# Where VectorE forms two low parts of the softmax weights, and the order of two jobs on GpSimd, in a two-layer cross-attention kernel

## Chip, core and metric

The kernel runs on one core of a Trainium2 chip. The metric is the device time of one execution in microseconds (us), from launch to end. The engines are TensorE (PE in the profile; its weight loads are PEld), VectorE (DVE), ScalarE (ACT), GpSimd (POOL) and SyncE (SP), which issues the DMAs.

## What is computed

Two transformer layers over x (8 batches x 512 tokens x 256). The change lies in the first attention of the second layer, a self-attention with 16 heads of 64:

```python
def _attn(xq, xc, Wq, Wk, Wv, Wo, bo):
    q = (xq @ Wq).reshape(B, N, HEADS, D_HEAD)
    k = (xc @ Wk).reshape(B, S, HEADS, D_HEAD)
    v = (xc @ Wv).reshape(B, S, HEADS, D_HEAD)
    scores = jnp.einsum("bnhd,bshd->bhns", q, k) * D_HEAD ** (-0.5)
    attn = jax.nn.softmax(scores, axis=-1)
    out = jnp.einsum("bhns,bshd->bnhd", attn, v).reshape(B, N, HEADS * D_HEAD)
    return out @ Wo + bo

x = _attn(_ln(x, g1, b1), _ln(x, g1, b1), Wq1, Wk1, Wv1, Wo1, bo1) + x      # L1, first attention
```

B is 8, N and S are 512, HEADS is 16, D_HEAD is 64. Before it runs layer L0 (cross-attention and an MLP), after it a second attention against the context and a gated MLP.

## The kernel before

**Precision.** Matmul operands are split in two: a rounded high part (`pool_copy` L159 on GpSimd or `act_copy` L156 on ScalarE) and a low part, source minus high part (`dve_rest` L162 on VectorE, `pool_rest` L165 on GpSimd). `mm3` (L146, L147, L148) sums high x high, high x low and low x high.

**Stage.** The self-attention is one software pipeline, `loop3`: s runs from -1 to 67, and N3 = 64 is the number of pairs of heads (8 batches x 8 pairs; pair p of batch b is step 8b + p). Step s works on three pairs: it projects pair u = s+1, forms scores and exponentials of pair t = s, and multiplies the weights of pair d = s-1 with the values. A step has four parts, j = 0 to 3. In part j the keys of block j (128 of 512) are handled: TensorE writes the scores of both heads (128 x 1024), ScalarE takes the exponential into one of two buffers, `pst3[j % 2]` (`exponent`, L1530), the high part goes to `P3[0][:, j]` and the low part to `P3[1][:, j]`. GpSimd rounds blocks 0 and 3, ScalarE blocks 1 and 2. VectorE's `rests(n)` forms the low part of block n = 4t + j; it reads two SBUF tensors of 128 x 1024 and signals `p3_lo`. The exponential of block n waits for `rests(n - 2)`, since it writes the same buffer; TensorE's `values(d, j)` waits for `rests(4d + j)`, and the next block's scores on TensorE wait for the exponential.

Also in step s, for pair u = s+1:

- j = 0: TensorE projects the queries (`project(u, 0)`, into bank 2) and the keys (`project(u, 1)`, bank 3). ScalarE copies the queries of head 0, takes exponential 4s, copies the queries of head 1, then the keys of each head. VectorE forms the low parts of queries (L1599, two instructions, the second after ScalarE's copy for head 1) and of keys (L1603, two). GpSimd copies the high keys once more (`k3_dup`, two copies 64 x 512).
- j = 1: values projected (`project_v`); ScalarE rounds them, VectorE's `value(u)` forms their low part from PSUM (128 x 256, two instructions).
- the row maxima: for each of four query blocks TensorE writes plain scores, and VectorE reduces them (`largest`, L1618, 128 x 1024 in PSUM, four in a step). On VectorE the order is block 0 in j = 1, blocks 1 and 2 in j = 2, block 3 in j = 3. On TensorE block 2 waits for the maximum of block 0 and block 3 for that of block 1, for their banks; block 1 waits for the low values; block 0 waits for the low keys.

For finished pairs: SyncE brings the sums of the exponentials of pair s-2 together, VectorE takes the reciprocal (L1647, in j = 0), and SyncE spreads it through DRAM. In j = 2 GpSimd multiplies the output of pair s-2 by it (L1734), rounds it (L159, 128 x 512) and forms its low part (L165, signal `o3_lo`). In j = 3 TensorE's `output` applies the output weights to half of the tokens for two pairs, into bank 2: it waits for `b3_max` of block 2 (whose maxima stood in banks 2 and 3), and in odd steps also for the `o3_lo` of the same step. VectorE adds the result to x (L1666), then bank 2 is free for the next `project(u, 0)`. In step p = 4 VectorE also takes the statistics of the next batch's layer norm, in p = 5 it scales, and in p = 6 TensorE transposes (L152; after the maximum of block 1), ScalarE applies the affine part, and GpSimd splits the result (`ln_split_pool`) before the next projection.

**Order.** Each engine executes its instructions in the order of the program; semaphores join the engines. The order is written by hand in `dve_attention1`, `pool_attention1` and the like.

Of the kernel before, what the change touches and what calls it, by code (L numbers as in the profile page):

```python
# [110 lines left out]
def build(nc, x, ctx_in, par, con, bias, wts, out):  # L111
    es = ExitStack()
    with es:  # L113
# [262 lines left out]
        def ok(v, n):  # L376
            return 0 <= v < n
# [925 lines left out]
        def out3_at(s, j):  # L1303

            e, half = (s - 2, 0) if s % 2 else (s - 3, 1)
            return [(e, half)] if ok(e, N3) and j == (1 if half and e >= N3 - 3 else 3) else []
# [285 lines left out]
        def dve_attention1():  # L1592
            def project(u, n):
                i, src = u % 2, bank(2 + n)
                for h in range(2):
                    hs = src[64 * h:64 * h + 64, :]
                    if n == 0:
                        dve.wait_ge(q3_hi, 2 * u + h)
                        nc.vector.tensor_tensor(qb[i][h][top, :], hs, f32(qa[i][h])[top, :], ALU.subtract  # L1599
                                                ).then_inc(q3_lo.sem, 1)  # L1600
                    else:
                        dve.wait_ge(k3_hi, 2 * u + h)
                        nc.vector.tensor_tensor(ka[i][h][low, :], hs, f32(ka[i][h])[top, :], ALU.subtract  # L1603
                                                ).then_inc(k3_lo.sem, 1)

            def rests(n):
                if 0 <= n < 4 * N3:
                    if n % 4 in (1, 2):
                        dve.wait_ge(p3_act, 2 * (n // 4) + n % 4 - 1)
                    else:  # L1610
                        dve.wait_ge(p3_pool, 2 * (n // 4) + n % 4 // 3)
                    dve_rest(P3[1][:, n % 4, :], pst3[n % 2], P3[0][:, n % 4, :]).then_inc(p3_lo.sem, 1)

            def largest(u, q, b0):
                dve.wait_ge(b3_mm, 4 * u + q)
                dve.wait_ge(nm3_mm, u - 1)
                dve.wait_ge(m3_set, 0)
                nc.vector.tensor_reduce(M3[:, q, 0:128:64], bank(b0, 2).rearrange("p (a b) -> p a b", a=2),  # L1618
                                        AX.X, ALU.max).then_inc(b3_max.sem, 1)

            def value(u):
                s_ = v3_s[(u // 2) % 2]
                src = bank(v3_bank(u)).rearrange("p (t a e) -> p t a e", t=2, a=2)
                tt = slice(2 * (u % 2), 2 * (u % 2) + 2)
                dve.wait_ge(v3_hi, u)
                for c in range(2):
                    cs = slice(128 * c, 128 * c + 64)
                    m = dve_rest(s_[1][:, tt, :, cs], src[:, :, :, 64 * c:64 * c + 64], s_[0][:, tt, :, cs])
                m.then_inc(v3_lo.sem, 1)

            ahead = dve_attention2()
            for s in loop3:
                t, u, d = s, s + 1, s - 1
                b, p = divmod(max(t, 0), 8)
                more = ok(t, N3)
                if s == 0:
                    after_attention0(dve)
                for j in range(4):
                    if j == 0:
                        rests(4 * s - 1)  # L1640
                    if ok(u, N3) and j == 0:
                        project(u, 0)
                    if ok(d - 1, N3) and j == 0:
                        k, i = (d - 1) % 2, (d - 1) // 2
                        dve.wait_ge(sum3[k], 2 * i + 1)
                        dve.wait_ge(out3[k], i - 1)
                        nc.vector.reciprocal(SR3[k], SQ3[k]).then_inc(rec3.sem, 1)  # L1647
                    if ok(u, N3) and j == 0:
                        project(u, 1)
                    if j == 1:  # L1650
                        rests(4 * s)
                    if s == 0 and j == 1:
                        value(0)
                    if ok(u, N3) and u > 0 and j == 1:
                        value(u)
                    if ok(u, N3) and j >= 2:
                        largest(u, 2 * j - 3, odd_bank(u))
                    if j == 2 or j == 3 and not out3_at(s, j):
                        rests(4 * s + j - 1)
                    for e, half in out3_at(s, j):  # L1660
                        xv = xbuf(2, e // 8)[:, 2 * half:2 * half + 2, :]
                        dve.wait_ge(o3_mm, e - 1 + half)
                        dve.wait_ge(x_bias, 16 + e // 8)
                        if e % 8 > 1:
                            dve.wait_ge(o3_add, e - 3 + half)
                        nc.vector.tensor_tensor(xv, bank(out3_bank(e, j)).rearrange("p (a c) -> p a c", a=2), xv, ALU.add  # L1666
                                                ).then_inc(o3_add.sem, 1)
                        if j == 3:
                            rests(4 * s + 2)
                    if ok(u, N3) and j in (1, 2):  # L1670
                        largest(u, 2 * j - 2, 2)
                    for job in weights3_at(s, j):
                        dve_weight_rest(job)
                    for _ in range(early4.get(tail3(s, j), 0)):
                        next(ahead)
                    if more and j == 3 and p == 4:
                        ln_x_stats(*after3(b))
                    if s < 0:
                        yield s
                if more and p == 5:  # L1680
                    ln_scale(18 + b, xbuf(*after3(b)), C)
            for _ in ahead:
                pass

        def pool_attention1():
# [1 line left out]
                nc.gpsimd.memset(f32(v3_s[i][0][:, :, :, 64:128]), 1.0)  # L1687
                nc.gpsimd.memset(f32(v3_s[i][1][:, :, :, 64:128]), 0.0).then_inc(v3_set.sem, 1)

            def rounded(t, j):  # L1690
                pool.wait_ge(e3, 4 * t + j)
                pool.wait_ge(d3_mm, 4 * (t - 1) + j)
                pool_copy(P3[0][:, j, :], pst3[j % 2]).then_inc(p3_pool.sem, 1)

            pool.wait_ge(x_out[x_at(0, 3)], store_no[0, 3])
            nc.gpsimd.memset(M3, 0.0).then_inc(m3_set.sem, 1)
            pool.wait_ge(o0_mm, 2 * NB - 1)
# [15 lines left out]
            for s in loop3:  # L1713
                t, u, d = s, s + 1, s - 1
                b, p = divmod(max(t, 0), 8)
                more = ok(t, N3)
                if s == 0:
                    after_attention0(pool)
                    ones(1)
                if s == 2:  # L1720
                    for b_ in (6, 7):
                        pool.wait_ge(x_out[x_at(0, b_)], store_no[0, b_])
                for j in range(4):
                    if ok(t, N3) and j == 0:
                        rounded(t, 0)
                    if ok(u, N3) and j == 0:
                        for h in range(2):
                            pool.wait_ge(k3_hi, 2 * u + h)
                            pool_copy(kb[u % 2][h][top, :], f32(ka[u % 2][h])[top, :]).then_inc(k3_dup.sem, 1)
                    if ok(d - 1, N3) and j == 2:  # L1730
                        f = d - 1
                        pool.wait_ge(in3[f % 2], 2 * (f // 2) + 1)
                        pool.wait_ge(d3_out, f)
                        nc.gpsimd.tensor_tensor(OA, OA, RS3, ALU.mult).then_inc(mul3.sem, 1)  # L1734
                        pool.wait_ge(mul3, f)
                        pool.wait_ge(o3_mm, 2 * ((f - 4) // 2) + 1)
                        pool_copy(o3_s[f % 4][0], OA).then_inc(o3_hi.sem, 1)
                        pool.wait_ge(o3_hi, f)
                        pool_rest(o3_s[f % 4][1], OA, o3_s[f % 4][0]).then_inc(o3_lo.sem, 1)
                    if ok(t, N3) and j == 3:  # L1740
                        rounded(t, 3)
                    for job in weights3_at(s, j):
                        pool_weight(job)
                    for _ in range(early4_pool.get(tail3(s, j), 0)):
                        next(ahead)
                    if j == 2 and more and p == 6:
                        pool.wait_ge(v3_mm, 8 * (b - 1) + 7)
                        ln_split_pool(18 + b, ns[(b + 1) % 2])
                    if more and j == 0 and p == 5:
                        ln_pool_rstd(18 + b)  # L1750
                    if s < 0:
                        yield s
                if more and p == 5:
                    ln_add(pool, *after3(b))
# [421 lines left out]
```

## Time and profile before

| | |
|---|---|
| time, median of 3 | 2228.43 us (2227.48 to 2229.39) |
| profiled execution | 2228.43 us, its span 2226.6 us |
| busy share over the span | PE 94%, PEld 80%, DVE 72%, ACT 67%, POOL 46% |
| mean granted TensorE clock | 0.985 of full speed |
| the self-attention stage | about 547 to 1690 us of the span |

The span runs from the first to the last instruction; the profiled execution's own time is 1.8 us more than its span. PE busy counts overlapping matmuls as one stretch. "Idle before" in a row is the time that the engine stood still ahead of the instruction, and the arrow names what released it.

### The profile page before, as it was taken

What the parts mean: (1) busy time and instruction counts of PE and PEld (TensorE: products, weight loads), DVE (VectorE), ACT (ScalarE), POOL (GpSimd) and SP (SyncE); (2) the same over time, 40 slices, a digit from 0 to 9 for tenths busy, and PEclk for the clock granted to TensorE, in tenths of its full rate; (3) what the DMA queues carried; (4) which work ended last, traced back from release to release, by engine and by line L of the source; (5) the groups of instructions that cost most, each with busy time, mean ns of one, the idle gap of its engine ahead of it and who ended that gap; (6) DMA issues with size and microseconds to landing.
All of it is one profiled execution on the core that took longest, in us unless ns stands there. A gap on an engine that the chain in (4) does not pass through costs nothing. (4 is left out here: it accounts for less than half of the span.)

```text
span 2226.6 us, 31299 instructions
## 1 busy us (share of the span) xinstructions
PE 2100.8 (94%) x11628; PEld 1777.8 (80%) x11628; DVE 1606.0 (72%) x2349; ACT 1486.7 (67%) x2157; POOL 1020.8 (46%) x830
## 2 busy tenths in 40 slices
PE   6868999999999999999999999999997799999998
PEld 4656888887778888888788888887876689898887
DVE  5567677665887878878878778887785866666543
ACT  5546788766778777777777777777774355455431
POOL 2146444440354454444544545345454666655422
PEclk9978999999999999999999999999999899999999
DMA  6910000011000100101001010010014411111000
GB/s 193 327 44 8 22 22 22 11 67 48 22 25 16 34 15 15 39 16 34 15 16 34 15 34 15 20 34 15 25 27 180 149 39 57 43 53 48 10 10 20
DMA packets 84280, 102.67 MB, mean 46 GB/s; under 512 B 29664, under 2 KB 61152, under 8 KB 83616
## 3 DMA queue, kind: packets, MB, share of 16 engines
q1 hardware_dynamic: 84128, 100.66, 13.9%
q8 instruction: 93, 1.52, 0.3%
q14 instruction: 59, 0.48, 0.1%
HBM read 65.50 MB, written 33.82 MB: 45 GB/s over the span
## 5 line engine op out<-in xcount | busy, mean ns | idle before, releaser
L146 PE MATMUL PS<-R 128*128 128x256 f32 (+1 forms) x2944 | 1025.3, 348 | 70.3 <-DVE R L162 23.9
L148 PE MATMUL PS<-R 128*128 128x256 f32 (+1 forms) x2944 | 995.7, 338 | 0.0
L147 PE MATMUL PS<-R 128*128 128x256 f32 (+1 forms) x2944 | 995.4, 338 | 0.0
L146 PEld LDWEIGHTS PS<-R 128*128 128x128 f32 x2944 | 562.9, 191 | 187.5 <-issue 53.4
L156 ACT ACTIVATE R<-PS 64x512 fp32r<-64x512 f32 (+4 forms) x860 | 459.7, 547 | 259.4 <-PE PS L1840 131.0
L148 PEld LDWEIGHTS PS<-R 128*128 128x128 f32 x2944 | 562.7, 191 | 60.3
L147 PEld LDWEIGHTS PS<-R 128*128 128x128 f32 x2944 | 563.5, 191 | 54.6
L159 POOL TENSOR_SCALAR R<-F 128x512 fp32r<-128x512 f32 (+1 forms) x293 | 304.1, 1039 | 454.2 <-ACT F L1530 275.2
L162 DVE TENSOR_TENSOR R<-F,R 128x1024 fp32r<-128x1024 f32 (+2 forms) x418 | 458.4, 1110 | 40.8 <-POOL R L159 24.0
L1618 DVE TENSOR_REDUCE F<-PS 128x2 f32<-128x1024 f32 x256 | 301.4, 1214 | 11.2 <-PE PS L1421 10.9
L1530 ACT ACTIVATE F<-PS 128x1024 f32<-128x1024 f32 x256 | 263.0, 1027 | 48.9 <-DVE R L162 27.0
L162 DVE TENSOR_TENSOR R<-PS,R 128x512 fp32r<-128x512 f32 (+3 forms) x348 | 180.8, 542 | 142.3 <-ACT R L156 139.7
L156 ACT ACTIVATE R<-F 128x1024 fp32r<-128x1024 f32 (+2 forms) x248 | 202.9, 832 | 103.3 <-PE PS L148 98.9
L165 POOL TENSOR_TENSOR R<-F,R 128x512 fp32r<-128x512 f32 (+2 forms) x124 | 195.8, 1581 | 24.2 <-ACT R L156 15.7
L156 ACT ACTIVATE F<-PS 64x512 f32<-64x512 f32 (+3 forms) x280 | 160.1, 593 | 69.9 <-PE PS L148 57.5
L1734 POOL TENSOR_TENSOR F<-F 128x512 f32<-128x512 f32 x64 | 87.6, 1369 | 246.7 <-DMA F<-sd 246.7
L1599 DVE TENSOR_TENSOR R<-PS,R 64x512 fp32r<-64x512 f32 x128 | 87.9, 687 | 125.7 <-ACT R L156 125.7
L1383 PE MATMUL PS<-R 128*128 128x512 f32 x512 | 165.6, 404 | 1.4 <-ACT R L156 1.4
L1421 PE MATMUL PS<-R 128*128 128x512 f32 x512 | 160.4, 395 | 6.9 <-ACT F L156 4.9
L1387 PE MATMUL PS<-R 128*128 128x512 f32 x512 | 159.8, 393 | 2.7 <-ACT R L156 2.7
L1170 POOL TENSOR_TENSOR F<-F 128x1024 f32<-128x1024 f32 x32 | 68.0, 2123 | 157.9 <-DVE F L1069 157.6
L1997 DVE SCALAR_TENSOR_TENSOR F<-PS,F 128x512 f32<-128x512 f32 x64 | 47.8, 747 | 102.8 <-PE PS L148 59.1
(92 smaller groups left out, 2032.7 us busy)
## 6 DMA issues: line engine op xcount, KB each, us to landing
F<-sd SPq DMA_DIRECT2D x128, 128.0 KB, 2.9
xs<-F SPq DMA_DIRECT2D x16, 512.0 KB, 3.5
F<-xs SPq DMA_DIRECT2D x16, 512.0 KB, 3.5
gd<-F SPq DMA_DIRECT2D x8, 768.0 KB, 3.9
vd<-F SPq DMA_DIRECT2D x8, 768.0 KB, 6.4
R<-gd SPq DMA_DIRECT2D x6, 1024.0 KB, 5.6
R<-vd SPq DMA_DIRECT2D x6, 1024.0 KB, 5.6
F<-in_x SPq DMA_DIRECT2D x8, 512.0 KB, 5.5
```

What stands on the lines that cost most here:

```text
L146: nc.tensor.matmul(o, L[0], Rr[0], start=start, stop=False, skip_group_check=share)
L147: nc.tensor.matmul(o, L[0], Rr[1], start=False, stop=False, skip_group_check=share)
L148: return nc.tensor.matmul(o, L[1], Rr[0], start=False, stop=stop, skip_group_check=share)
L156: return nc.scalar.activation(o, i, ACT.Identity, **k)
L159: return nc.gpsimd.tensor_scalar(o, i, 1.0, 1.0, ALU.mult, ALU.mult)
L162: return nc.vector.tensor_tensor(o, i, f32(hi), ALU.subtract)
L165: return nc.gpsimd.tensor_tensor(o, i, f32(hi), ALU.subtract)
L1383: nc.tensor.matmul(bank(h), ka[i][h][:, kk], qa[i][h], start=True, stop=False)
L1387: m = nc.tensor.matmul(bank(h), kb[i][h][:, kk], qb[i][h], start=False, stop=True)
L1421: m = nc.tensor.matmul(bank(b0 + h), qa[i][h][:, 128 * q:128 * q + 128], ka[i][h], start=True, stop=True)
L1530: nc.scalar.activation(pst3[n % 2], bank(0, 2), ACT.Exp, scale=0.125).then_inc(e3.sem, 1)
L1618: nc.vector.tensor_reduce(M3[:, q, 0:128:64], bank(b0, 2).rearrange("p (a b) -> p a b", a=2), AX.X, ALU.max).then_inc(b3_max.sem, 1)
```

## The change

On VectorE, in part j = 0, `rests(4s - 1)` no longer comes first: it comes after `project(u, 0)` and the reciprocal, ahead of `project(u, 1)`. In part j = 1 `rests(4s)` no longer comes ahead of `value(u)` but after it, ahead of the first `largest`. On GpSimd the helper `rounded` is written out in place, and the rounding of block 0 comes after the two copies of the keys instead of ahead of them. The number of instructions and all waits stay the same.

```diff
@@ dve_attention1 @@
                 for j in range(4):
-                    if j == 0:
-                        rests(4 * s - 1)
                     if ok(u, N3) and j == 0:
                         project(u, 0)
                     if ok(d - 1, N3) and j == 0:
...
                         nc.vector.reciprocal(SR3[k], SQ3[k]).then_inc(rec3.sem, 1)
+                    if j == 0:
+                        rests(4 * s - 1)
                     if ok(u, N3) and j == 0:
                         project(u, 1)
-                    if j == 1:
-                        rests(4 * s)
                     if s == 0 and j == 1:
                         value(0)
                     if ok(u, N3) and u > 0 and j == 1:
                         value(u)
                     if ok(u, N3) and j >= 2:
                         largest(u, 2 * j - 3, odd_bank(u))
-                    if j == 2 or j == 3 and not out3_at(s, j):
+                    if j in (1, 2) or j == 3 and not out3_at(s, j):
                         rests(4 * s + j - 1)
@@ pool_attention1 @@
-            def rounded(t, j):
-                pool.wait_ge(e3, 4 * t + j)
-                pool.wait_ge(d3_mm, 4 * (t - 1) + j)
-                pool_copy(P3[0][:, j, :], pst3[j % 2]).then_inc(p3_pool.sem, 1)
@@
                 for j in range(4):
-                    if ok(t, N3) and j == 0:
-                        rounded(t, 0)
                     if ok(u, N3) and j == 0:
                         for h in range(2):
                             pool.wait_ge(k3_hi, 2 * u + h)
                             pool_copy(kb[u % 2][h][top, :], f32(ka[u % 2][h])[top, :]).then_inc(k3_dup.sem, 1)
...
-                    if ok(t, N3) and j == 3:
-                        rounded(t, 3)
+                    if ok(t, N3) and j in (0, 3):
+                        pool.wait_ge(e3, 4 * t + j)
+                        pool.wait_ge(d3_mm, 4 * (t - 1) + j)
+                        pool_copy(P3[0][:, j, :], pst3[j % 2]).then_inc(p3_pool.sem, 1)
```

## Rows read from the trace of the kernel before

**Rows 1.** Windows, three steps in turn: length, busy (instructions), clock, DMA share, GB/s.

```profile
900.04:917.26 17.22, 17.22 (x89) 14.49 (x88) 13.87 (x17) 13.37 (x20) 7.38 (x7) 1.00 0.15 47
917.26:935.09 17.83, 17.44 (x89) 14.38 (x88) 15.73 (x26) 14.14 (x22) 8.32 (x8) 1.00 0.07 16
935.09:955.06 19.97, 18.74 (x97) 15.16 (x97) 15.83 (x21) 15.42 (x24) 13.12 (x10) 1.00 0.06 15
```

**Rows 2.** Waits of TensorE from 600 to 1600 us: total us, times, longest.

```profile
PE PS L146 <- POOL R L165: 14.0, 28, 1.2
```

**Rows 3.** Timeline of VectorE in the first of these steps: start, us, instruction.

```profile
899.90 2.35 DVE L162 TENSOR_TENSOR R<-F,R 128x1024 fp32r<-128x1024 f32 x2
...
905.84 0.19 DVE L1647 RECIPROCAL F<-F 128x8 f32<-128x8 f32 x1
906.06 1.41 DVE L1603 TENSOR_TENSOR R<-PS,R 64x512 fp32r<-64x512 f32 x2
907.50 1.23 DVE L162 TENSOR_TENSOR R<-F,R 128x1024 fp32r<-128x1024 f32 x1
908.75 0.76 DVE L162 TENSOR_TENSOR R<-PS,R 128x256 fp32r<-128x256 f32 x2
909.43 2.35 DVE L1618 TENSOR_REDUCE F<-PS 128x2 f32<-128x1024 f32 x2
911.69 1.62 DVE L162 TENSOR_TENSOR R<-F,R 128x1024 fp32r<-128x1024 f32 x1
913.24 2.34 DVE L1618 TENSOR_REDUCE F<-PS 128x2 f32<-128x1024 f32 x2
```

**Rows 4.** Timeline of ScalarE in the same step.

```profile
906.45 1.03 ACT L1530 ACTIVATE F<-PS 128x1024 f32<-128x1024 f32 x1
907.37 0.65 ACT L156 ACTIVATE R<-PS 128x256 fp32r<-128x256 f32 x2
```

**Rows 5.** Timeline of GpSimd in the same step.

```profile
905.89 1.24 POOL L159 TENSOR_SCALAR R<-R 64x512 fp32r<-64x512 f32 x2 [0.79 <-ACT R L156]
910.94 1.29 POOL L1734 TENSOR_TENSOR F<-F 128x512 f32<-128x512 f32 x1 [3.82 <-DMA F<-sd]
```

**Rows 6.** Timeline of TensorE, the three steps.

```profile
900.04 0.50 PE L146 MATMUL PS<-R 128*128 128x512 f32 x1
...
914.87 0.28 PE L146 MATMUL PS<-R 128*128 128x256 f32 x1
...
932.64 0.36 PE L146 MATMUL PS<-R 128*128 128x256 f32 x1 [0.39 <-POOL R L165]
...
955.06 0.50 PE L146 MATMUL PS<-R 128*128 128x512 f32 x1 [0.62 <-POOL R L165]
```

**Rows 7.** Timeline of VectorE in the third step (p = 6).

```profile
942.58 1.54 DVE L162 TENSOR_TENSOR R<-F,R 128x1024 fp32r<-128x1024 f32 x1
...
947.08 1.21 DVE L162 TENSOR_TENSOR R<-F,R 128x1024 fp32r<-128x1024 f32 x1
...
953.57 0.69 DVE L1666 TENSOR_TENSOR F<-PS,F 128x512 f32<-128x512 f32 x1 [1.60 <-PE PS L148]
954.17 1.91 DVE L162 TENSOR_TENSOR R<-F,R 128x1024 fp32r<-128x1024 f32 x1
```

**Rows 8.** Timeline of GpSimd in the third step.

```profile
941.85 1.19 POOL L159 TENSOR_SCALAR R<-R 64x512 fp32r<-64x512 f32 x2
947.17 2.27 POOL L1734 TENSOR_TENSOR F<-F 128x512 f32<-128x512 f32 x1 [4.13 <-DMA F<-sd]
...
950.23 1.30 POOL L165 TENSOR_TENSOR R<-F,R 128x512 fp32r<-128x512 f32 x1
...
952.62 2.38 POOL L165 TENSOR_TENSOR R<-F,R 128x1024 fp32r<-128x1024 f32 x1
954.96 2.03 POOL L159 TENSOR_SCALAR R<-F 128x1024 fp32r<-128x1024 f32 x1
```

**Rows 9.** Timeline of VectorE at the stage's end (step 64).

```profile
1689.62 0.20 DVE L1647 RECIPROCAL F<-F 128x8 f32<-128x8 f32 x1 [3.68 <-DMA F<-F]
```

## Prediction

> **What bounds the kernel now.** I read the page first (PE 94% busy), then the windows of single steps of the self-attention, because the change touches only that stage. The even step has 17.22 us, all of it with PE busy; the odd one 17.83 us, with PE busy for 17.44; the layer-norm step (p = 6) 19.97 us [rows 1]. The chain of waits shows what PE lacks in an odd step: the low part of the attention output from POOL, 14.0 us in 28 waits over 1000 us, 0.5 us each [rows 2]. So the stage is bound by PE in even steps, by PE and POOL's chain in odd ones. DVE is busy for 13.87 us of 17.22, with 3.3 us to spare; that average says nothing of where the spare time lies, so I went to the timeline.
>
> I write times in a step as +x, counted from the first matmul of the query projection, which stands at 900.04 [rows 6]. DVE does two rests on end at 899.90 [rows 3]; the second is `rests(4s-1)`. It falls in a hole: from its end at 902.25 to the reciprocal at 905.84 DVE has only the two short query rests, for which it waits on ScalarE's copies. From the reciprocal (+5.80) to the last maximum (915.58, +15.54) DVE then has no idle time in its rows [rows 3]. The maximum of block 2 ends near 914.4 (+14.4), and PE starts `output`, which needs it, at 914.87, +14.83 [rows 3, 6]: 0.4 us of slack, less the signal. Behind `output` come DVE's add and the next query projection, 17.22 - 14.83 = 2.39 us later [rows 1, 6]. This is a loop: projection, ScalarE's copies, DVE's run of work, `output`, add, projection.
>
> **The change, part by part.** Nothing is added or removed; the cost is in the order.
>
> *`rests(4s-1)`* leaves the hole and enters the unbroken run, ahead of the key rests. It costs 1.2 us there if it runs freely (1.23 at 907.50 [rows 3]). The hole that it leaves gives nothing back: the second query rest and the reciprocal go by ScalarE. *`rests(4s)` after `value(u)`* is a swap within the run. It makes no work, but the low values are wanted after ScalarE's rounding, which follows exponential 4s+1, and that waits for `rests(4s-1)`.
>
> *A lock between DVE and POOL* sets the rest of the price. In the third step the rest at 942.58 took 1.54 us, and it ended (944.12) 1.08 us after POOL's second key copy (943.04); the rest at 954.17 took 1.91 and ended 1.08 us after POOL's low part of 952.62 (955.00) [rows 7, 8]. In the other direction POOL's product at 947.17 took 2.27 us against 1.29 in the first step, and ended 1.15 us after the DVE rest that had begun before it (948.29) [rows 5, 7, 8]. So a rest from two SBUF tensors and a POOL instruction exclude each other, whichever is first, and the later one loses the overlap. At 955.00 both waited, and DVE went ahead of POOL's next instruction (954.96, 2.03 us) [rows 7, 8]. The key rests at 906.06, which read PSUM, overlap POOL's key copies and aren't stretched: 1.41 us for two of 64 x 512 [rows 3, 5]. The Trainium skill ("SBUF — State Buffer", Who interferes with whom) says that a DVE instruction with two SBUF inputs and a GpSimd instruction that reads SBUF lock each other out for the whole instruction; these rows agree. Without such a rule the time would be the one that I give as the third rival.
>
> Now one even step with the new order:
>
> - +6.02, after the reciprocal: `rests(4s-1)` is ready, but POOL's first key copy runs from 905.89 (+5.85) for 0.6 us [rows 5], so the rest runs from +6.45 to +7.53 (1.08).
> - Key rests (1.41 [rows 3]): +7.56 to +8.97; before, they ended at +7.43. PE's first plain scores wait for them, about 0.5 us.
> - Exponential 4s+1 waits for the rest: +7.63 to +8.66 (1.03), then the rounding of the values (0.65, starting 0.1 before the end) to +9.20 [rows 4]. It began at +6.41 before.
> - `value(u)`: +9.24 to +10.0 (0.76); `rests(4s)`: +9.92 to +11.13 (1.22). POOL's rounding of block 0, now behind the key copies (end +8.05, the second copy being held by the rest) takes 1.05 and ends at +9.15, so this edit costs nothing; its cover is the 0.8 us before +9.92.
> - POOL's product wants to start at +10.90 [rows 5], its time hanging on the reciprocal and the DMAs alone, which aren't moved. It is locked out until +11.13. From the like case [rows 7, 8] its low part starts 950.23 - 948.29 = 1.94 us after the DVE rest's end: +13.07, until +14.37.
> - Two maxima: from +11.05, 2.26 us until the next instruction may start (909.43 to 911.69 [rows 3]): `rests(4s+1)` is ready at +13.31. POOL was first by 0.24 us. It waits until +14.37, ends at +15.45.
> - Maximum of block 2: 1.15 us more, +16.6. `output` can start at +16.65, the next projection 2.42 us on (2.39 in the even, 935.09 - 932.64 = 2.45 in the odd step [rows 1, 6]): a step of 19.07 us.
>
> Nothing else is later than that: PE, held at the scores too, would be at `output` by +15.6; the last exponential ends 1.1 us after `rests(4s+1)`, at +16.6, and what ScalarE does behind it is wanted only in the next step, by TensorE's values. `o3_lo` comes at +14.4 and no longer holds odd steps, so both kinds last 19.07: +1.85 and +1.24.
>
> *The p = 6 step*: PE's transposes wait for the maximum of block 1, +12.1 before and +13.4 after. The next projection was held there by POOL (955.06); by the add alone (953.57 + 0.74) it could have come at 954.31, 0.75 us earlier [rows 6, 7]. So the 1.3 us make 0.55.
>
> *The end*: in step 64 DVE waits 3.68 us for a DMA ahead of the reciprocal [rows 9], and `rests(255)`, until now ahead of it, falls behind; the last values wait. I take 2 us, once (bounds 0 and 1.2 + 3.7 = 4.9).
>
> Sum over steps 1 to 62: 23 even x 1.85 = 42.6, 31 odd x 1.24 = 38.4, 8 with p = 6 x 0.55 = 4.4, the end 2: +87 us. The profiled execution's time, 2228.43 (span 2226.6 and 1.8 around it), is the median of the runs too, so 2228.4 + 87 = 2315 us. The likeliest case's own range is 2300 to 2330: each 0.1 us in the +16.65 is 5.4 us over 54 steps. What I can't bound well is who gets the lock.
>
> **The rivals.**
>
> *DVE wins the lock at `rests(4s+1)`.* The lead of POOL is only 0.24 us. If DVE comes first, its rest ends at +14.4 and POOL's low part at +15.7; the maximum of block 2 is there at +15.6. Steps of 18.07 (even) and 18.15 (odd): 23 x 0.85 + 31 x 0.32 + 4.4 + 2 = +36, 2264 us. For it: if the first rest isn't held by the key copy, `rests(4s)` ends at +10.7, the product runs free from +10.9, its low part starts at +12.98, and `rests(4s+1)` is ready at +12.88. Against it: both sides count from the same DVE end, by durations that repeat.
>
> *DVE loses to both key copies* at +6.45 (they follow each other without a gap). Then the whole run is 0.62 us later: 54 x 0.62 = +33 more, 2348 us. Against it stands the handover at 955.00 [rows 7, 8].
>
> *No lock matters*: the run is longer by a rest and the wait for the values only. `output` at +15.5, steps of 17.9: 23 x 0.7 + 31 x 0.1 + 4.4 + 2 = +26, 2254 us.
>
> *The order hides it, and it is faster.* With `rests(4s+1)` later, POOL's rounding and low part of the output aren't held, `o3_lo` comes 0.8 us earlier, and PE's 0.5 us waits in odd steps go: 14.0 us in 56 steps, 16 in 64 [rows 2], 2212 us. It decides if the maximum of block 2 is delayed by less than the 0.4 us of slack; I find 1.2 at least, from one rest's length alone. If gain and delay cancel, no change.
>
> **How the numbers follow.** Chances: the likeliest case 0.50, DVE wins the lock 0.17, no lock 0.08, both key copies 0.08, hidden and faster 0.06, no change 0.07, anything slower than all of these 0.04. 2315 us is the likeliest. The range 2248 to 2336 holds the first three (0.75) and the parts of the others that lie between them. About 0.2%, 4.5 us, is what a measurement here can tell from no change: faster 0.06, same 0.07, slower 0.87.
>
> **What would show it.** In the new trace: steps of about 19.1 us, odd and even alike; the rest after the reciprocal at 1.5 us instead of 1.2; POOL's product stretched by 0.2; `rests(4s+1)` at 2.1 us instead of 1.62, with POOL's low part under its start; PE idle of about 1 us ahead of `output`, released by DVE L1618 and no longer by POOL L165; no idle of DVE between the reciprocal and the last maximum beyond the 0.25 for the values. Steps of 18.1 would show the first rival. The forecast is wrong if the reciprocals keep their 17.2 and 17.8 us distance, or if PE's waits are at ScalarE's exponentials instead.

## The result, and the profile after

The changed kernel takes 2247.89 us (2247.59 to 2248.1, 4 runs) against 2228.86 for the kernel before: ratio 1.0086, interval 1.0068 to 1.0104, or +19 us. Slower, as forecast, but +87 us was forecast, and 2247.9 lies just below the range. The profiled execution took 2249.57 us with a span of 2247.8, 21.2 more than before.

Windows of the same three steps (20, 21, 22) of the changed kernel; columns as in [rows 1]:

```profile
906.87:924.60 17.73, 17.70 (x89) 14.25 (x88) 13.34 (x17) 13.51 (x21) 8.46 (x7) 1.00 0.16 45
924.60:942.51 17.91, 17.75 (x89) 14.24 (x89) 15.19 (x26) 13.93 (x21) 9.39 (x8) 1.00 0.05 16
942.51:962.54 20.03, 18.99 (x97) 15.03 (x97) 14.81 (x21) 14.83 (x22) 14.07 (x10) 1.00 0.06 15
```

The even step has 17.73 us instead of 17.22; in these windows the odd one and the p = 6 step hardly changed. I had forecast 19.07 for both ordinary kinds. The distances of the reciprocals (L1647 before, L1645 after) give the means over steps 2 to 61. They stand at these places before, first and last of the 61 that bound those steps:

```profile
586.04 0.19 DVE L1647 RECIPROCAL F<-F 128x8 f32<-128x8 f32 x1
...
1656.10 0.19 DVE L1647 RECIPROCAL F<-F 128x8 f32<-128x8 f32 x1
```

and after:

```profile
587.93 0.19 DVE L1645 RECIPROCAL F<-F 128x8 f32<-128x8 f32 x1
...
1674.59 0.19 DVE L1645 RECIPROCAL F<-F 128x8 f32<-128x8 f32 x1
```

Even steps: 17.25 to 17.79 us (23 of them), odd 17.93 to 17.91 (30), p = 6 19.36 to 20.02 (7). That is 12.6 - 0.6 + 4.6 = 16.6 us, the whole of 1086.66 - 1070.06. The stage's start adds 1.9 (587.93 against 586.04), and what lies behind 1674.59 the rest, 2.7: 1.9 of it up to the stage's last addition to x (1732.56 before, 1752.93 after), 0.8 behind it, where nothing was moved. The p = 6 mean hides something: step 22, the one in these windows and in [rows 1], went only from 19.95 to 20.00, the other six from 19.27 to 20.02.

VectorE in the even step after, its matmuls starting at 906.87; for [rows 3]:

```profile
912.66 0.19 DVE L1645 RECIPROCAL F<-F 128x8 f32<-128x8 f32 x1
912.77 1.17 DVE L162 TENSOR_TENSOR R<-F,R 128x1024 fp32r<-128x1024 f32 x1
913.97 1.41 DVE L1603 TENSOR_TENSOR R<-PS,R 64x512 fp32r<-64x512 f32 x2
915.64 0.76 DVE L162 TENSOR_TENSOR R<-PS,R 128x256 fp32r<-128x256 f32 x2 [0.26 <-ACT R L156]
916.32 1.22 DVE L162 TENSOR_TENSOR R<-F,R 128x1024 fp32r<-128x1024 f32 x1
917.45 2.35 DVE L1618 TENSOR_REDUCE F<-PS 128x2 f32<-128x1024 f32 x2
919.71 1.22 DVE L162 TENSOR_TENSOR R<-F,R 128x1024 fp32r<-128x1024 f32 x1
920.85 2.35 DVE L1618 TENSOR_REDUCE F<-PS 128x2 f32<-128x1024 f32 x2
```

GpSimd in it, for [rows 5], and TensorE's `output`, for [rows 6]:

```profile
912.71 2.29 POOL L159 TENSOR_SCALAR R<-R 64x512 fp32r<-64x512 f32 x2 [7.28 <-ACT R L156]
...
917.80 1.29 POOL L1725 TENSOR_TENSOR F<-F 128x512 f32<-128x512 f32 x1 [1.80 <-DMA F<-sd]
919.18 0.63 POOL L159 TENSOR_SCALAR R<-F 128x512 fp32r<-128x512 f32 x1
919.89 2.20 POOL L165 TENSOR_TENSOR R<-F,R 128x512 fp32r<-128x512 f32 x1
```

```profile
922.12 0.39 PE L146 MATMUL PS<-R 128*128 128x256 f32 x1
```

TensorE's first plain scores, and its last matmul ahead of `output`, before:

```profile
908.51 0.62 PE L1421 MATMUL PS<-R 128*128 128x512 f32 x2
...
914.64 0.39 PE L148 MATMUL PS<-R 128*128 128x512 f32 x1
```

and after:

```profile
915.53 0.70 PE L1421 MATMUL PS<-R 128*128 128x512 f32 x2
...
921.82 0.39 PE L148 MATMUL PS<-R 128*128 128x512 f32 x1
```

And TensorE's waits from 600 to 1600 us, for [rows 2]; the second line is that of the transposes in the p = 6 steps, and isn't in the list of before:

```profile
PE PS L146 <- POOL R L165: 2.6, 7, 0.7
PE PS L152 <- DVE F L1618: 2.8, 7, 0.4
```

What the reader is to see: the moved rest (912.77) takes 1.17 us, so it isn't held; it is GpSimd's pair of key copies that grew from 1.24 [rows 5] to 2.29. The run ends earlier than I had it: `rests(4s)` at +10.67 (917.54) instead of +11.13, GpSimd's product starts freely at +10.93, and `rests(4s+1)` starts at 919.71 (+12.84), 0.18 us *ahead* of GpSimd's low part (919.89), which now waits (2.20 instead of 1.29). `output` starts at 922.12, +15.25, not +16.65. Before, it was +14.83 [rows 6]. TensorE's waits for GpSimd's low parts went from 14.0 us [rows 2] to 2.6.

TensorE lost the 0.51 us in parts, as its rows tell. The low keys now end at +8.51 instead of +7.43, and the first plain scores, which need them, start at +8.66 instead of +8.47. At the last matmul ahead of `output` TensorE is 0.35 us late (+14.95 against +14.60), and at `output` 0.42. So the late low keys and the late maximum of block 2 (its row ends near +15.15) hold TensorE almost equally. None of it appears as idle time ahead of `output`: the window has TensorE busy for 17.70 of 17.73 us. The window's busy share doesn't show these waits.

### The profile page after: what moved, and what is told of

Its sections match the earlier page's. It is cut to its first block and busy times, and to the rows that moved or that the text cites. A ratio compares the mean times of both kernels' runs of the same rounds, so it can differ in the third digit from the quotient of the medians.

```text
span 2247.8 us, 31299 instructions
## 1 busy us (share of the span) xinstructions
PE 2123.8 (94%) x11628; PEld 1767.0 (79%) x11628; DVE 1572.2 (70%) x2349; ACT 1485.5 (66%) x2157; POOL 1079.4 (48%) x830
## 5 line engine op out<-in xcount | busy, mean ns | idle before, releaser
L162 DVE TENSOR_TENSOR R<-F,R 128x1024 fp32r<-128x1024 f32 (+2 forms) x418 | 430.0, 1033 | 36.3 <-POOL R L159 21.4
L159 POOL TENSOR_SCALAR R<-F 128x512 fp32r<-128x512 f32 (+1 forms) x293 | 255.0, 872 | 201.6 <-DVE F L1990 147.7
L159 POOL TENSOR_SCALAR R<-R 64x512 fp32r<-64x512 f32 x128 | 144.2, 1140 | 411.5 <-ACT R L156 411.5
L165 POOL TENSOR_TENSOR R<-F,R 128x512 fp32r<-128x512 f32 (+2 forms) x124 | 249.6, 2015 | 23.8 <-ACT R L156 15.4
L1421 PE MATMUL PS<-R 128*128 128x512 f32 x512 | 167.5, 409 | 9.7 <-ACT F L156 4.9
L1383 PE MATMUL PS<-R 128*128 128x512 f32 x512 | 166.6, 406 | 2.0 <-ACT R L156 1.4
L1387 PE MATMUL PS<-R 128*128 128x512 f32 x512 | 160.7, 395 | 1.9 <-ACT R L156 1.9
L1725 POOL TENSOR_TENSOR F<-F 128x512 f32<-128x512 f32 x64 | 82.7, 1292 | 124.1 <-DMA F<-sd 124.1
```

What stands on the lines that cost most here:

```text
L159: return nc.gpsimd.tensor_scalar(o, i, 1.0, 1.0, ALU.mult, ALU.mult)
L162: return nc.vector.tensor_tensor(o, i, f32(hi), ALU.subtract)
L165: return nc.gpsimd.tensor_tensor(o, i, f32(hi), ALU.subtract)
L1383: nc.tensor.matmul(bank(h), ka[i][h][:, kk], qa[i][h], start=True, stop=False)
L1387: m = nc.tensor.matmul(bank(h), kb[i][h][:, kk], qb[i][h], start=False, stop=True)
L1421: m = nc.tensor.matmul(bank(b0 + h), qa[i][h][:, 128 * q:128 * q + 128], ka[i][h], start=True, stop=True)
```

## Experiments

Every time is compared with runs of the kernel before on the same chip, whose medians were 2228.63 us beside experiment 1, 2225.88 beside experiment 2, late_by_a_quarter and reciprocal_early, and 2227.53 beside the other three.

**1. The parts of the change, one by one.**

```diff
 rest3_only: before, and rests(4s - 1) behind the reciprocal
 swap_only:  before, and rests(4s) behind value(u)
 pool_only:  before, and GpSimd's rounded(t, 0) behind the key copies
 both_dve_moves: rest3_only and swap_only together
```

Expected of rest3_only: 

> The kernel before with one part of the change: rests(4s-1) behind the reciprocal. Theory (the run of VectorE from the second query rest to the maximum of block 2 grows by one rest of 1.17 us, of which some 0.5 us is slack before TensorE's output projection; VectorE wins the lock against GpSimd): most of the loss comes from here. Even steps 17.65 to 17.8 us, odd ones 17.8 to 17.9, p = 6 at 20.0; time +15 to +19 us over the kernel before. Rival A (the loss comes from the swap of rests(4s) and the low values, by later exponentials): +0 to +4. Rival B (from the order on GpSimd): +0 to +4.

Expected of swap_only: 

> The kernel before with only rests(4s) behind value(u). Theory: VectorE waits 0.55 us for ScalarE's rounding of the values, so the first two maxima come 0.4 us later, and rests(4s+1) then waits less for the lock that GpSimd's product holds until +12.19; the maximum of block 2 is where it was. +0, within 2 us. Rival A: +15 or more. Rival B: +0.

Expected of pool_only: 

> The kernel before with only GpSimd's order changed (key copies ahead of the rounding of block 0). Theory: the rounding ends at +8.15 instead of +5.1, and rests(4s), wanted at +7.46, waits 0.7 us for it; the maximum of block 2 comes at +15.2: even steps 17.6 to 17.7, odd ones as before; +8 to +12 us, though the same edit costs nothing within the change. Rival (the order on GpSimd is free by itself too): +0 to +2.

Expected of both_dve_moves: 

> The changed kernel with GpSimd's order as before. Theory: in the changed order VectorE wants the rounding of block 0 only at +9.4, after +8.15, so GpSimd's order makes no difference: +19 us over the kernel before, within 2 us of the changed kernel's 2247.9. Rival B (the loss comes from GpSimd's order): 2229 to 2235.

| kernel | median us | ratio (interval) | even / odd / p = 6 step |
|---|---|---|---|
| rest3_only | 2263.30 | 1.0157 (1.0141 to 1.0174) | 18.14 / 18.15 / 20.02 |
| swap_only | 2231.48 | 1.0014 (1.0003 to 1.0024) | 17.27 / 18.03 / 19.28 |
| pool_only | 2247.46 | 1.0090 (1.0075 to 1.0105) | 17.72 / 18.01 / 19.59 |
| both_dve_moves | 2246.91 | 1.0086 (1.0070 to 1.0103) | 17.76 / 17.93 / 20.03 |

The parts don't add up. The moved rest alone costs +35 us, nearly twice the whole change, and my +15 to +19 was wrong. The waits of TensorE in rest3_only, 600 to 1600 us (total, times, longest), say why:

```profile
PE PS L1421 <- DVE R L162: 17.6, 54, 0.3
```

In 54 steps, 0.33 us each, TensorE's scores for the maximum of block 1 wait for the low values, since `value(u)` now stands behind two rests. In the changed kernel this wait isn't there: the swap puts `value(u)` ahead of `rests(4s)` and takes back 16 us (2263.3 to 2246.9). So the swap, a loss of 3 us by itself where I expected at most 2, is a repair of the first move. GpSimd's order costs +19 us alone, where +8 to +12 was expected. The even steps are near what I expected (17.72 where I had 17.6 to 17.7), the odd and p = 6 steps rise too. The place of the wait is the same as in rest3_only:

```profile
PE PS L1421 <- DVE R L162: 10.8, 54, 0.2
```

Within the change GpSimd's order costs nothing, where 2246.91 and 2247.89 are the same: VectorE no longer wants block 0 so early.

**2. How full is the hole, and what does the run cost?** An added maximum (128 x 1024 from SBUF, 1.15 us) at either place:

```diff
+                    if n % 4 == 3:     # dose_in_hole; n % 4 == 0 in dose_in_run
+                        nc.vector.tensor_reduce(J[:, n // 4:n // 4 + 1], pst3[n % 2][:, 0:1024], AX.X, ALU.max)
                     dve_rest(P3[1][:, n % 4, :], pst3[n % 2], P3[0][:, n % 4, :]).then_inc(p3_lo.sem, 1)
```

Expected of dose_in_hole: 

> The kernel before with 64 more VectorE instructions, a maximum over one 128 x 1024 SBUF tensor into a spare column (about 1.15 us each, one SBUF input), each directly ahead of rests(4s-1), in the hole at the start of the step. Theory (the hole is 2 us wide, and what stands in it costs nothing): +0 to +2 us. Rival (VectorE's total work sets the time): about the same loss as the same instruction elsewhere, 10 us or more.

Expected of dose_in_run: 

> The same 64 instructions, directly ahead of rests(4s), inside VectorE's unbroken run. Theory: the run is 1.15 us longer with no lock involved; even steps 17.6 to 17.8 us, odd ones about as before: +14 to +20 us, as the change. Rival (the change's loss needs the late low parts of block 3 or the lock on the moved rest): +5 or less.

dose_in_hole took 2247.53 us (1.0094, 1.0081 to 1.0108), +22, and the "+0 to +2" was wrong. But the loss sits in few steps: steps 2 and 3 still have 17.19 and 17.69 us, while steps 12 and 13 (p = 4 and 5) have 17.91 and 19.08, against 17.22 and 17.72 before. Over steps 2 to 61 the 16 with p = 4 or 5 lose 19.9 us, the seven with p = 6 gain 2.8, and the other 37 lose 0.9 together: there the hole is free. Behind p = 4 it isn't empty. VectorE there (line numbers are one or three higher in these kernels):

```profile
920.69 1.40 DVE L241 BATCH_NORM_STATS2 F<-F 128x6 f32<-128x256 f32 x4
922.13 0.38 DVE L245 BATCH_NORM_AGGREGATE F<-F 128x2 f32<-128x6 f32 x4
922.54 0.17 DVE L250 TENSOR_SCALAR F<-F 128x4 f32<-128x4 f32 x1
922.62 1.21 DVE L1614 TENSOR_REDUCE J<-F 128x1 f32<-128x1024 f32 x1
923.75 2.07 DVE L163 TENSOR_TENSOR R<-F,R 128x1024 fp32r<-128x1024 f32 x1
```

The layer norm's statistics fill it, and the rest comes so late that GpSimd's rounding of block 0 is 0.05 us ahead of it; so the rest also takes 2.07 us:

```profile
923.70 1.05 POOL L160 TENSOR_SCALAR R<-F 128x1024 fp32r<-128x1024 f32 x1 [5.02 <-ACT F L1531]
```

dose_in_run took 2266.47 us (1.0185, 1.0169 to 1.0200), +41, where I had expected +14 to +20. It has the same wait as rest3_only, larger:

```profile
PE PS L1422 <- DVE R L163: 35.2, 54, 0.7
```

So 1.15 us in the run ahead of the values costs about twice what it costs in the hole, the ordinary steps pay all alike (18.16 us in the even, 18.24 in the odd ones), and the rival "total work of VectorE decides" doesn't hold. The expectation had nothing for the values, which stand behind the added work.

**3. Would the predicted chain exist if GpSimd won the lock?** A short maximum between the reciprocal and the moved rest, on the changed kernel, 128 x 192 from SBUF, then the same from PSUM:

```diff
+                    if n % 4 == 3:
+                        nc.vector.tensor_reduce(J[:, n // 4:n // 4 + 1], pst3[n % 2][:, 0:192], AX.X, ALU.max)  # late_by_a_quarter
+                        nc.vector.tensor_reduce(J[:, n // 4:n // 4 + 1], bank(2)[:, 0:192], AX.X, ALU.max)      # late_psum_source
                     dve_rest(...)   # cut short; each kernel has one of the two lines
```

Expected of late_by_a_quarter: 

> The changed kernel with a short VectorE maximum (128 x 192, about 0.26 us) between the reciprocal and rests(4s-1), so that the rest comes about 0.25 us after the start of GpSimd's first key copy instead of 0.06 us after it. Theory (GpSimd now has the lock, and with it the chain that I had predicted for the change: the rest at 1.4 to 1.5 us, rests(4s) up to +11.1, the product held, GpSimd's low part ahead of rests(4s+1)): steps near 19.0 us, time +80 to +90 us over the kernel before. Rival 1 (the copy is short and VectorE loses only its 0.35 us once): steps 18.0 to 18.3, +35 to +45. Rival 2 (VectorE still has the lock; only 0.25 us more of work): steps 17.9 to 18.0, +25 to +32.

Expected of late_psum_source: 

> As the run late_by_a_quarter, but the short maximum reads PSUM (128 x 192) instead of SBUF. In late_by_a_quarter the rest still went ahead of GpSimd's key copy, whose row had begun 0.28 us earlier (rows 5.85 and 6.13). Theory R (the reciprocal and the short maximum, SBUF to SBUF, held the lock without a gap until the rest): now GpSimd's first copy gets through at about +6.0 with 0.6 us, the rest is blocked and takes 1.4 us or more, and the first copy's duration is 0.6 to 0.75 us instead of 1.97. Theory S (the lock is decided otherwise, for example by when the instruction is queued): the first copy again takes 1.9 to 2.0 us and the rest 1.2. In time: S as late_by_a_quarter, 2290 to 2305; R 2300 to 2325.

2299.29 us (1.0325, 1.0311 to 1.0340) and 2315.84 us (1.0395, 1.0379 to 1.0412): +73 and +88 over the kernel before. The changed kernel has +19 of it, so 0.22 and 0.39 us of more work in a step cost 54 and 69 us, where 54 x 0.39 is 21. The first lies below the +80 to +90 of the theory. VectorE, then GpSimd in a step of late_by_a_quarter that starts at 923.60:

```profile
929.72 1.21 DVE L163 TENSOR_TENSOR R<-F,R 128x1024 fp32r<-128x1024 f32 x1
...
936.70 2.26 DVE L163 TENSOR_TENSOR R<-F,R 128x1024 fp32r<-128x1024 f32 x1
```

```profile
929.44 2.55 POOL L160 TENSOR_SCALAR R<-R 64x512 fp32r<-64x512 f32 x2 [7.14 <-ACT R L157]
...
936.58 1.30 POOL L166 TENSOR_TENSOR R<-F,R 128x512 fp32r<-128x512 f32 x1
```

The first lock still goes to VectorE, so that part of the theory failed: the rest (929.72) isn't stretched, and the copies are, although the first copy's row begins 0.28 us before. The second lock has turned: GpSimd's low part starts 0.12 us ahead of `rests(4s+1)`, which takes 2.26 us. The steps fall into two kinds, near 18.0 and near 19.0 us, mostly the latter (mean 18.75): one lock, won or lost.

The same of late_psum_source, a step that starts at 929.06, with TensorE's `output` and next projection:

```profile
935.35 1.24 DVE L163 TENSOR_TENSOR R<-F,R 128x1024 fp32r<-128x1024 f32 x1
...
938.96 1.22 DVE L163 TENSOR_TENSOR R<-F,R 128x1024 fp32r<-128x1024 f32 x1
...
942.36 2.14 DVE L163 TENSOR_TENSOR R<-F,R 128x1024 fp32r<-128x1024 f32 x1
```

```profile
934.90 2.16 POOL L160 TENSOR_SCALAR R<-R 64x512 fp32r<-64x512 f32 x2 [7.26 <-ACT R L157]
...
942.12 1.30 POOL L166 TENSOR_TENSOR R<-F,R 128x512 fp32r<-128x512 f32 x1
```

```profile
945.69 0.39 PE L147 MATMUL PS<-R 128*128 128x256 f32 x1 [0.86 <-DVE F L1621]
...
948.18 0.50 PE L147 MATMUL PS<-R 128*128 128x512 f32 x1
```

Here `rests(4s)` ends at 940.18, +11.12; the low part starts at +13.06, `rests(4s+1)` at +13.30 and ends at +15.44, `output` starts at +16.63, and the step has 19.12 us. The prediction had +11.13, +13.07, +13.31, +15.45, +16.65 and 19.07. So everything behind `rests(4s)` in the predicted schedule was right, for a kernel in which `rests(4s)` ends there; in the changed kernel it ends 0.46 us earlier. The pair of copies took 2.16 us, against 2.55 with the SBUF source: the first now ran in 0.61 us, to 935.51, and the second waited for the rest. The rest ended 1.08 us after 935.51, as behind a copy in [rows 7, 8], so it was held; but it had come only 0.16 us before that end and lost next to nothing (1.24). So "1.4 us or more" failed, except in an early step where the rest came sooner. GpSimd, then VectorE there:

```profile
588.41 2.16 POOL L160 TENSOR_SCALAR R<-R 64x512 fp32r<-64x512 f32 x2 [6.67 <-ACT R L157]
```

```profile
588.68 1.42 DVE L163 TENSOR_TENSOR R<-F,R 128x1024 fp32r<-128x1024 f32 x1
```

**4. What the hole is worth to another instruction.** The same hole can take the reciprocal, which starts GpSimd's chain.

```diff
@@ reciprocal_early @@
                     if j == 0:
                         rests(4 * s - 1)
-                    if ok(u, N3) and j == 0:
-                        project(u, 0)
                     if ok(d - 1, N3) and j == 0:
...
                         nc.vector.reciprocal(SR3[k], SQ3[k]).then_inc(rec3.sem, 1)
+                    if ok(u, N3) and j == 0:
+                        project(u, 0)
@@ rec_early_product_waits, also on GpSimd, ahead of the product @@
+                        if ok(t, N3):
+                            pool.wait_ge(p3_lo, 4 * t)
                         pool.wait_ge(in3[f % 2], 2 * (f // 2) + 1)
```

change_on_rec_early is the changed kernel with the reciprocal ahead of `project(u, 0)`.

Expected of reciprocal_early: 

> The kernel before with one other move: the reciprocal ahead of project(u, 0), behind rests(4s-1), so in the hole. Theory: the sums' DMAs are issued at -1.7 us of the step and have landed by then; GpSimd's product, rounding and low part of the output come about 3.5 us earlier, TensorE no longer waits 0.5 us for o3_lo in odd steps, odd steps go from 17.9 to 17.25: -15 to -24 us against the kernel before. Rival 1 (the sums land too late, VectorE waits for them ahead of the query rests): odd steps stay or the time rises. Rival 2 (the product now collides with rests(4s) for the lock and lengthens VectorE's run): even steps longer, +-5 us in all.

Expected of rec_early_product_waits: 

> The kernel reciprocal_early, with GpSimd's product waiting for rests(4s). In reciprocal_early a step has 17.20 us where the product starts at +8.6, and 17.97 where it starts at +7.43, 0.07 us ahead of rests(4s), which then takes 2.30 us. Theory (that lock is all that keeps even and odd steps above 17.2): all ordinary steps near 17.2 to 17.3 us, time 2205 to 2213. Rival (the later product makes rests(4s+1) or o3_lo late): steps 17.5 or more, no better than reciprocal_early (2219.5).

Expected of change_on_rec_early: 

> The changed kernel with the reciprocal ahead of project(u, 0). Theory (VectorE's run is longer by a rest whatever the reciprocal does, and the product, now wanted before +9.2, starts right behind the rounding of block 0 and ahead of rests(4s), which is blocked): steps 18.2 to 18.6 us, 2265 to 2295. Rival (the earlier reciprocal gives the change its slack back): 2225 to 2248.

reciprocal_early took 2219.46 us (0.9963, 0.9951 to 0.9976), -6 us where -15 to -24 was expected, and rival 2 was half right. Some steps lose a lock; VectorE, then GpSimd in one that does:

```profile
885.72 2.30 DVE L162 TENSOR_TENSOR R<-F,R 128x1024 fp32r<-128x1024 f32 x1
```

```profile
885.65 1.29 POOL L1734 TENSOR_TENSOR F<-F 128x512 f32<-128x512 f32 x1 [0.20 <-DMA F<-sd]
```

The product came 0.07 us ahead of `rests(4s)`, and `rests(4s)` took 2.30 us. With GpSimd's wait for `rests(4s)` this can't be, and rec_early_product_waits took 2207.53 us (2207.08 to 2209.4; 0.9912, 0.9899 to 0.9924), 20 us less than the kernel before and 40 less than the changed one. Its ordinary steps, even and odd, nearly all have 17.2 us (those with p = 5 up to 17.6), and of TensorE's waits from 600 to 1600 us one kind is left:

```profile
PE PS L1421 <- ACT F L156: 4.3, 7, 0.6
```

change_on_rec_early took 2295.60 us (1.0305, 1.0288 to 1.0321), 76 us more than reciprocal_early and just above the expected range: ordinary steps mostly of 18.5 us. VectorE, then GpSimd in one of its steps:

```profile
913.25 2.05 DVE L162 TENSOR_TENSOR R<-F,R 128x1024 fp32r<-128x1024 f32 x1
```

```profile
912.93 1.29 POOL L1725 TENSOR_TENSOR F<-F 128x512 f32<-128x512 f32 x1
```

The early product comes 0.32 us ahead of the late `rests(4s)`, as expected, and the change costs four times as much as on the kernel before.

## Why the prediction was wrong

Right: the sign, and its reason. The moved rest leaves a hole where it was free in ordinary steps and joins a run that TensorE waits for. The maximum of block 2 sets the even step, though only by about 0.1 us over TensorE's own hold at the low keys; odd steps have their slack from GpSimd's chain, and `o3_lo` seldom holds them. The order on GpSimd costs nothing within the change (both_dve_moves against the changed kernel), and the end costs 1.9 us where I took 2.

Right by luck: the p = 6 step, with +0.66 us where +0.55 was forecast. I had taken 0.75 us off the 1.3, for a wait on GpSimd ahead of the next projection that step 22 has (0.62 us at 955.06 [rows 6]). It is the only one of the seven with that wait. It grew by 0.05 us, the other six by 0.75; with nothing taken off, the forecast for those six would have been +1.3. By luck too the third rival, "no lock matters", has the nearest number, 2254 us: the pair of copies (2.29 for 1.24) and GpSimd's low part (2.20 for 1.29) show the lock at work, in VectorE's favour.

Wrong, and it is one step: "`rests(4s-1)` is ready, but POOL's first key copy runs from 905.89 (+5.85) for 0.6 us, so the rest runs from +6.45 to +7.53". The rest ran from 912.77 (+5.90) to +7.07. Two readings were off. I let it start behind the reciprocal's end (+6.02), but the rows of the changed kernel overlap by 0.08 us. And I took the start of GpSimd's row as the moment at which it has the lock; the rest, starting 0.06 us later, went first. The second is the one that counted: in late_by_a_quarter the rest came 0.28 us later and still went first. Its 0.46 us wouldn't have been much: 54 x 0.46 is 25 us. But everything behind it was built on a lead of 0.24 us at the second lock, and 0.46 us turned it round. Thus +19.07 became 17.73: the product ran free, `rests(4s+1)` was first, and 1.85 us in an even step became 0.51 to 0.55, 1.24 in an odd one became nothing. late_psum_source, with `rests(4s)` at +11.12, shows the chain as forecast, and 2315.84 us.

The first rival named this course, with its condition ("if the first rest isn't held by the key copy, `rests(4s)` ends at +10.7", product +10.9, low part +12.98, `rests(4s+1)` +12.88; measured +10.67, +10.93, +13.02, +12.84), and was then priced with the other one's +11.13: 18.07 us a step, 2264 us. From its own +10.7 the maximum of block 2 is ready at +15.2 and the even step has 17.7, the odd one its old time; 23 x 0.51 + 8 x 0.6 + 2 gives 18 to 19 us. A rival has to be worked out from its own condition.

What none of the cases held: that `value(u)` is as pressing as the maxima. I called the swap "a swap within the run". rest3_only shows that without it the loss would have been +35.

Not settled: what let VectorE have the first lock. As a rule the rows do tell who is first. In the traces of all thirteen kernels, from 500 to 1720 us, I find 582 cases in which a rest directly follows a VectorE instruction that reads PSUM and its row starts between 0.03 and 0.3 us before or after that of a GpSimd instruction (leaving out rests that an earlier GpSimd instruction holds already, and GpSimd's 128 x 4 power). In every one the earlier row won and the other was stretched. The first lock is the exception: directly behind the reciprocal (changed kernel, 0.06 us) or the short SBUF maximum (late_by_a_quarter, 0.20 to 0.28) the rest beat the copy that was ahead of it. With the maximum from PSUM the copy won, but there the rest also came later, by 0.43 to 0.45 us, so source and lead changed together; only the early step at 588.41, with a lead of 0.27 us, speaks for the source alone. Against a plain rule "an SBUF instruction just ahead keeps the lock" stands dose_in_hole: directly behind an SBUF maximum and 0.05 us behind GpSimd's rounding the rest was held (2.07).

## What to carry to other kernels

Before moving an instruction, ask what the place it leaves was good for: a hole in which the engine waits anyway is worth most to whatever starts a long chain on another engine (here the reciprocal), and an instruction taken out of it must be paid for in the run behind. Where two engines exclude each other, a schedule is only as good as the smallest lead in it. Here a lead of 0.18 us turned round with 0.22 us of more work: work out both courses of such a lead to the end, or fix the order by a wait, as rec_early_product_waits did. Before taking a cost from one step, look whether its neighbours of the same kind have the same waits. Parts of a reordering don't add up, so a part that looks useless alone may be what keeps the rest cheap.

## What the runs showed of the hardware

A rest and a large GpSimd instruction (64 x 512 to 128 x 1024) never overlapped by more than 0.24 us with both at full speed, in any of these kernels; the one that was late paid the other's remainder: rests of 1.17 to 1.23 us took 2.14 to 2.30 in the rows above, a pair of copies of 1.24 took 2.16 to 2.55. That agrees with what the Trainium skill says in "SBUF — State Buffer", Who interferes with whom: an exclusive lock, held for the whole instruction, by issue order. One small instruction differs from "the whole instruction": GpSimd's power over 128 x 4 elements (L259, 924.33 to 925.34 in the kernel before) had a rest under it for 0.60 us, and the rest was not stretched (1.23). A rest behind the end of the instruction that held it took 1.08 us more, a held copy of 64 x 512 0.47, a held GpSimd product or low part of 128 x 512 1.15 or 1.16. The starts of the rows told who was first down to 0.03 us, but not at the first lock, where the rest directly behind the reciprocal or the short SBUF maximum went first from up to 0.28 us behind. A DVE instruction's row can start up to 0.09 us before the end of the one ahead of it.
